# Moving the attention-times-values products one group later and laying the step of a fused transformer block out anew

## The reference, cut to what matters

```python
# x: (16, 56, 56, 32) f32; windows of 7 x 7 after a roll by 3; 4 heads of 8
q, k, v = split(ln(x) @ w_qkv + b_qkv); q = q * 8 ** -0.5      # ln over the 32 channels
attn = softmax(q @ k.T) + bias[head] + mask[window]            # the bias comes after the softmax
x = x + (attn @ v) @ w_proj + b_proj                           # rolled back
probs = softmax(ln(x) @ router_w + router_b)                   # 8 experts
top_p, top_i = top_k(probs, 2); top_p = top_p / sum(top_p)
x = x + sum over the 2 picked experts e of top_p[e] * (ln(x) @ expert_w[e] + expert_b[e])
```

## Time and profile before

| what | value |
|---|---|
| median of 3 runs | 817.04 us (816.79, 817.04, 819.18) |
| the profiled execution: its time | 821.02 us |
| its span, first to last instruction | 819.2 us |
| mean granted clock of TensorE in it | 0.940 of full speed |
| busy in the span | PE 83%, DVE 66%, POOL 63%, PEld 54%, ACT 47% |

### The profile page before, as it was taken

One profiled execution on the slowest core, in us unless ns is written; L12 is line 12 of the kernel. 1 busy time (PEld: TensorE's weight loads), 2 busy tenths in 40 slices (PEclk: granted clock), 3 DMA queues, 4 the chain that ended last, 5 costly groups with the idle time before them and its releaser, 6 DMA issues.

```text
span 819.2 us, 29441 instructions
## 1 busy us (share of the span) xinstructions
PE 677.5 (83%) x12632; PEld 443.1 (54%) x12632; DVE 544.2 (66%) x1003; ACT 387.3 (47%) x641; POOL 516.6 (63%) x555
## 2 busy tenths in 40 slices
PE   0777877979798989989798989989897989878675
PEld 0455554656556655645656565656556556645331
DVE  7352557867676767758676767768686667676544
ACT  1645462646464564636454554646464455612100
POOL 4736677586867768584868767685857666551520
PEclk9999898999999999979999999999998999987777
DMA  2000030313122130413131130413131030403040
GB/s 71 20 22 3 25 77 22 81 42 81 32 62 51 38 85 23 91 32 80 33 70 42 42 82 22 97 26 81 42 82 41 22 81 10 93 2 80 20 99 20
DMA packets 16961, 41.48 MB, mean 51 GB/s; under 512 B 9280, under 2 KB 9408, under 8 KB 15296
## 3 DMA queue, kind: packets, MB, share of 16 engines
q1 hardware_dynamic: 16240, 38.59, 21.2%
q10 hardware_dynamic: 592, 1.01, 0.4%
HBM read 7.47 MB, written 6.42 MB: 17 GB/s over the span
## 4 chain that ended last, share of the span: by engine, by line
PE 56%; DVE 23%; issue 11%; ACT 5%; POOL 4%; ACTq 0%; DVEq 0%; POOLq 0%
DVE mx L874 8%; PE ps_win L1210 7%; PE ps_acc L1310 6%; PE ps_shared L1136 6%; PE ps_weight L1293 5%; PE ps_win L1181 5%; PE ps_pv L1225 5%; PE ps_shared L1163 5%; PE ps_shared L1246 4%; DVE zt L989 4%; PE ps_shared L1147 3%; PE ps_win L1204 3%; DVE x L915 2%; DVE ms L888 2%; PE ps_acc L1305 2%
## 5 line engine op out<-in xcount | busy, mean ns | idle before, releaser
L874 DVE TENSOR_REDUCE mx<-ps_win 128x32 f32<-128x1568 f32 x64 | 114.5, 1789 | 66.5 <-PE ps_win L1181 65.9
L989 DVE TENSOR_TENSOR zt<-ps_weight,x 128x392 f32<-128x392 f32 x118 | 66.2, 561 | 83.0 <-PE ps_weight L1293 82.4
L1225 PEld LDWEIGHTS ps_pv<-vb,pt 128*49 128x49 f32 x4096 | 103.4, 127 | 14.5 <-issue 12.1
L777 ACT ACTIVATE pt<-ps_win 128x1568 f32<-128x1568 f32 x64 | 94.6, 1478 | 33.0 <-PE ps_win L1210 32.5
L611 POOL TENSOR_TENSOR on<-on,obs 128x256 f32<-128x256 f32 x64 | 46.6, 728 | 98.2 <-DVE on L901 72.6
L1225 PE MATMUL ps_pv<-vb,pt 128*49 128x18 f32 x4096 | 108.3, 200 | 0.0
L1293 PE MATMUL ps_weight<-wt,const_bf_tile 96*128 96x392 bf16 x234 | 82.3, 352 | 28.0 <-DVE zt L989 19.5
L989 DVE TENSOR_TENSOR x<-ps_weight,x 128x392 f32<-128x392 f32 x116 | 65.5, 564 | 33.3 <-PE ps_weight L1293 32.3
L768 ACT COPY mr<-ps_win 128x512 bf16<-128x512 bf16 x64 | 37.4, 584 | 87.7 <-PE ps_win L1189 87.7
L590 POOL TENSOR_TENSOR st<-st,minus_half 112x28 f32<-112x28 f32 x16 | 77.0, 4812 | 1.3
L557 POOL TENSOR_TENSOR st<-st,minus_half 112x28 f32<-112x28 f32 x16 | 76.9, 4809 | 1.3
(11 more groups left out here) (141 smaller groups left out, 1369.1 us busy)
## 6 DMA issues: line engine op xcount, KB each, us to landing
x<-x SPq DMA_DIRECT2D x48, 392.0 KB, 5.1
x<-x2t SPq DMA_DIRECT2D x64, 98.0 KB, 2.2
xin<-x SPq DMA_DIRECT2D x32, 150.0 KB
out<-xo SPq DMA_DIRECT2D x32, 150.0 KB
xin<-x SPq DMA_DIRECT2D x32, 18.0 KB
out<-xo SPq DMA_DIRECT2D x30, 18.0 KB
xin<-x SPq DMA_DIRECT2D x32, 15.6 KB
xin<-x SPq DMA_DIRECT2D x32, 1.9 KB
```

What stands on the lines that cost most here:

```text
L777: nc.scalar.activation(pt[g % 2].rearrange("p a x h n -> p a (x h n)"), ps_win[:, :, 0:2 * HN], ACT.Exp).then_inc(probs_ready, 1)
L874: nc.vector.tensor_reduce(mx[g % 2].rearrange("n a x h -> n a (x h)"), ps_win[:, :, 0:8 * N].rearrange("n a (k m) -> n a k m", m=N), AX, A ...
L989: nc.vector.tensor_tensor(tokens if eh else zt[:, a, :], weight_bank(w, 1 + i)[:, 0:HALF], tokens, ALU.mult).then_inc(weight_drained, 1)
L1225: ins = mm(ps_pv[PAD * x:PAD * x + N, c0:c0 + SLOT], pt[g % 2][:, a, x, h, :], vb[u.par][:, 2 * g + x, a, h, :], start=True, stop=True)
```

## The change

The values' products of group g-1 are put between the scores of group g and the next maximum; those of group 3 go into the next unit's first group, and the last unit's stand ahead of the tail. The place (g, 1) is now behind these products, (g, 2) behind the maximum. The work in `SIDE_TASKS` and in `TAIL` is dealt out anew. `ps_acc` becomes a second shared bank: nine of the users (`ON_ACC`) and the two sums take turns on it, and each waits only for the user before it on its own bank. The sum of the experts, which had the bank to itself, now waits for that user too. No instruction is added or left out, and none changes its shape.

```diff
@@ the places of the side work
-    (0, 0): [("ot", 1), ("keep", 0), ("wt", 0), ("y", 0), ("mix", 0), ("back", 0), ("mix", 1), ("y", 1), ("back", 1), ("norm2_center", 0)],
-    (0, 1): [("xt", 0), ("mix", 2)],
-    (0, 2): [],
-    (0, 3): [("mix", 3), ("norm2_square", 0), ("xt", 1), ("mix", 4), ("norm2_scale", 0)],
-    (1, 0): [("qk", 0), ("load", 0), ("mix", 5)],
-    (1, 1): [("qk", 1), ("mix", 6)],
-    (1, 2): [],
-    (1, 3): [("mix", 7), ("qk", 2)],
-    (2, 0): [("mix", 8), ("x2t", 0), ("norm1_center", 0), ("mix", 9)],
-    (2, 1): [("x2t", 1), ("mix_drain", 0)],
-    (2, 2): [("replicate", 0), ("kmask", 0), ("mix", 10), ("router", 0), ("mix", 11), ("qk", 3), ("place", 0), ("mix", 12), ("place", 1)],
-    (2, 3): [("top2", 0), ("mix", 13), ("kmask", 1), ("top2", 1), ("v", 0), ("top2", 2)],
-    (3, 0): [("top2_exp", 0), ("mix", 14), ("top2", 3), ("v", 1), ("mix", 15), ("top2", 4)],
-    (3, 1): [("top2", 5), ("mix", 16), ("ob", 0), ("mix_drain", 1)],
-    (3, 2): [],
-    (3, 3): [("norm1_square", 0), ("final", 0), ("top2", 6), ("top2", 7), ("ot", 0), ("final", 1), ("ob", 1), ("store", 0), ("norm1_scale", 0)],
+    (0, 0): [],
+    (0, 1): [("wt", 0), ("ot", 1), ("mix", 0), ("y", 0), ("back", 0), ("y", 1), ("back", 1), ("norm2_center", 0)],
+    (0, 2): [("xt", 0), ("xt", 1), ("qk", 0), ("mix", 1)],
+    (0, 3): [("norm2_square", 0), ("qk", 1), ("mix", 2), ("keep", 0)],
+    (1, 0): [("norm2_scale", 0), ("mix", 3)],
+    (1, 1): [("load", 0), ("kmask", 0), ("mix", 4)],
+    (1, 2): [("qk", 2), ("mix", 5)],
+    (1, 3): [("norm1_center", 0), ("mix", 6)],
+    (2, 0): [("mix", 7), ("x2t", 0), ("mix", 8)],
+    (2, 1): [("mix", 9)],
+    (2, 2): [("norm1_square", 0), ("mix_drain", 0), ("x2t", 1), ("mix", 10), ("qk", 3), ("router", 0), ("mix", 11), ("v", 0)],
+    (2, 3): [("top2", 0), ("mix", 12), ("place", 0), ("norm1_scale", 0), ("mix", 13), ("mix", 14)],
+    (3, 0): [("top2", 1), ("replicate", 0), ("mix", 15), ("top2", 2)],
+    (3, 1): [("place", 1), ("mix", 16), ("mix_drain", 1)],
+    (3, 2): [("v", 1), ("final", 0), ("ot", 0), ("top2_exp", 0)],
+    (3, 3): [("kmask", 1), ("top2", 3), ("top2", 4), ("top2", 5), ("final", 1), ("top2", 6), ("ob", 0), ("store", 0), ("ob", 1), ("top2", 7)],
@@ the banks
+SUM_STARTS = {5: 0, 13: 1}
+ON_ACC = {("ot", 1), ("xt", 1), ("qk", 0), ("y", 1), ("ot", 0), ("qk", 3), ("qk", 1), ("v", 0), ("ob", 1)}
@@ the tail
-TAIL = ((1, 1), (0, 1), (1, 6), (0, 1), (1, 1), (0, 11), (1, 2), (0, 1), (1, 1), (0, 1), (1, 1), (0, 1), (1, 3), (0, 1), (1, 1), (0, 2), (1, 2), (0, 4), (2, 2), (1, 1), (2, 5), (1, 1), (2, 5), (1, 1), (2, 12))
+TAIL = ((0, 1), (1, 1), (0, 1), (1, 7), (0, 12), (1, 3), (0, 2), (1, 1), (0, 2), (1, 1), (0, 1), (1, 1), (0, 1), (1, 3), (0, 3), (1, 1), (2, 1), (1, 2), (2, 4), (1, 1), (2, 19))
@@ macro_step
         yield "scores", att, g
         yield from side((g, 0))
+        unit, k = (att, g - 1) if g else (post, GROUPS - 1)
+        if unit is not None:
+            yield "pv", unit, k
+        yield from side((g, 1))
         unit, k = (att, g + 1) if g + 1 < GROUPS else (ahead, 0)
         if unit is not None:
             yield "maximum", unit, k
-        yield from side((g, 1))
-        yield "pv", att, g
         yield from side((g, 2))
@@ program, behind the last macro step
+    yield "pv", unit[UNITS - 1], GROUPS - 1
@@ TensorE: the wait before a bank is filled again
-            def shared_free(name, u, i):
+            def bank_free(name, u, i):
...
+                    if on_acc(other, j) != on_acc(name, i):
+                        continue
...
+                    if other == "sum":
+                        pe.wait_ge(sum_drained, upto("sum_drained", w, j))
+                        return
@@ TensorE: the start of a sum in mix
                 if eh == 0:
-
+                    if w.number >= UNITS - 2:
+                        tail_banks_free()
+                    else:
+                        bank_free("sum", w, half)
```

More of the change, by code:

```diff
@@ L97, with bank_order, on_acc @@
+def bank_order():
+    for place in sorted(SIDE_TASKS):
+        for name, i in SIDE_TASKS[place]:
+            if name in SHARED_BANK:
+                yield name, i
+            elif name == "mix" and i in SUM_STARTS:
+                yield "sum", SUM_STARTS[i]
+BANK_ORDER = list(bank_order())
+def on_acc(name, i):
+    return name == "sum" or (name, i) in ON_ACC
 PROLOGUE = (
@@ L474, in metaformer_block, with shared_bank, ot_bank @@
         rel_list = list(rel_loads())
+        def shared_bank(name, i):
+            return ps_acc if on_acc(name, i) else ps_shared
+        def ot_bank(u, i):
+            return ps_shared if u.number == UNITS - 1 and i else shared_bank("ot", i)
         def pre_bank(v, fill):
-            return ps_weight if v.number == 0 and fill % 2 else ps_shared
+            if v.number == 0:
+                return ps_weight if fill % 2 else ps_shared
+            return shared_bank(*PRE_NAMES[fill])
         def weight_bank(w, fill):
@@ L489, in token_bank @@
         def token_bank(w, fill):
-            spare = w.number == UNITS - 1 and fill in (1, 3)
-            return ps_win[:, 3, :] if spare else ps_shared
+            if w.number == UNITS - 1:
+                return ps_win[:, 3, :] if fill in (1, 3) else ps_shared
+            return shared_bank(*TOKEN_NAMES[fill])
         block = ctx.enter_context(nc.Block())
@@ L1093, in keep_awake @@
                     mm(ps_win[:, 0, :], identb, const_bf16_tile[:, 0:512], start=True, stop=True)
-            def shared_free(name, u, i):
-                at = SHARED_ORDER.index((name, i))
-                for back in range(1, 2 * len(SHARED_ORDER)):
-                    lap, k = divmod(at - back, len(SHARED_ORDER))
-                    before, j = SHARED_ORDER[k]
-                    w = u.moved(lap - later(name, i) + later(before, j))
-                    if w is not None:
-                        kind, first = SHARED_BANK[before]
-                        drained = {"pre": pre_drained, "ot": ot_drained, "token": token_drained}[kind]
+            def bank_free(name, u, i):
+                at = BANK_ORDER.index((name, i))
+                for back in range(1, 2 * len(BANK_ORDER)):
+                    lap, k = divmod(at - back, len(BANK_ORDER))
+                    other, j = BANK_ORDER[k]
+                    if on_acc(other, j) != on_acc(name, i):
+                        continue
+                    w = u.moved(lap - later(name, i) + later(other, j))
+                    if w is None:
+                        continue
+                    if other == "sum":
+                        pe.wait_ge(sum_drained, upto("sum_drained", w, j))
+                        return
+                    kind, first = SHARED_BANK[other]
+                    drained = {"pre": pre_drained, "ot": ot_drained, "token": token_drained}[kind]
+                    if kind == "pre" and w.number == 0:
+                        pe.wait_ge(pre_drained, upto("pre_drained", w))
+                    else:
@@ L1112, in token_free @@
                 else:
[L1113 removed]
+                    pe.wait_ge(token_drained, upto("token_drained", w, 3 if name == "router" else 1))
             def pre_free(v, i, fill):
@@ L1265, in router @@
             def router(w, _):
-                shared_free("router", w, 0)
+                token_free("router", w, 0)
+                bank = token_bank(w, 4)
                 pe.wait_ge(token_drained, upto("token_drained", w, 3))
                 for k in range(WS):
-                    ins = mm(ps_shared[0:ROWS, 32 * k:32 * k + 32], x2t[:, ROWS * k:ROWS * k + ROWS],
+                    ins = mm(bank[0:ROWS, 32 * k:32 * k + 32], x2t[:, ROWS * k:ROWS * k + ROWS],
                              wr[:, :, :].rearrange("p a e -> p (a e)"), start=True, stop=True)
```

33 lines of the change are left out of this document (22 added, 11 removed).

## The result

The changed kernel takes **921.4 us** in the median of 4 runs (910.17 to 927.36) against 817.12 before: 1.1228 times as long, interval 1.1171 to 1.1286. The direction was forecast, the size was not: 104 us longer instead of 6, far outside the range of 807 to 836. The ratio compares the means of the fast executions and leaves out the profiled one of the changed kernel, the slowest of its four (927.36 us, span 925.6, mean granted clock 0.869 for 0.881 and more in the others). Set against the span before, 819.2, the profiled execution is 106.4 longer, and the starts of the macro steps split that up: first start 0.9 earlier, units 0 and 1 together 100.3 for 80.2 (**+20.1**), units 2 to 14 673.0 for 594.1 (**+78.9**, 6.1 per step), from the start of unit 15 on 114.7 for 106.4 (**+8.3**).

What follows compares the result with a forecast made beforehand. The prediction took PE (TensorE) as the bound, busy 39.28 and 39.71 us of steps of 44.24 or 44.87. Steps +10.4, head -4 and tail -0.5 gave +5.9 on the median 817.04: 823.0 us, range 807 to 836.

Steps and rivals of the forecast that it cites:

- with 1.79 and the split the shift comes at 12.05: Group 0 on DVE: `mx` starts near 9.4, takes 1.79, then the split; PE waits 0.6 for DVE.
- three losses again: Clock: three of the 13 steps lose the full rate as before, with 4.66 us for one such step.
- The clock is lost more often: Rival, chance 0.10: idle stretches of group 0 follow one another, three more steps lose 4.66 us each, 837 us.
- The walk: One step in the new order with old durations: groups 0 to 3 +0.7, -0.4, +0.7, -0.2; +0.8 us per step.
- The queues: Engine queues that steps are moved past: POOL at worst 0.3 us late, priced at nothing, 13 x 0.5 in the range.
- the late picking: POOL's last picking step ends 4 us into the next step, where `wt` needs it; priced at nothing.
- The load: SP issues it 14 us into the step; it lands at about 20, just ahead of its reduction at about 20.3.
- The banks: Second shared bank: beyond the 0.25 us of `y` 1 it takes away no wait; priced at 0.
- The head: Units 0 and 1, without `mix`: products help in the exponentials' wait; -4 us, from -7 to 0.
- The tail: End of the kernel: `y` 2.3 us later, filling matmuls some 1.8 earlier; -0.5 us in all, from -3 to +3.

Runs made afterwards that it cites:

- run 1: The changed kernel with one wait added, so that POOL's `keep` starts only after DVE's split of group 1's maxima: 866.77 us, ratio 1.0594.
- run 2: The kernel before with `keep` held back until `mx` of group 1 is taken, so it starts with the split: 899.69 us, ratio 1.0978.
- run 7: The kernel before with users moved to the sum's bank: five users 850.78 us, ratio 1.0383; `y` 1 alone 828.90, ratio 1.0101.
- run 4: The changed kernel with maximum 1 ahead of `wt`, `ot` and `y`: 834.11 us; its last kernel, with `keep` also waiting for the split: 831.38.

## Why the prediction was right or wrong

**The step that failed** is in group 0: "with 1.79 and the split the shift comes at 12.05". It took the split at its old duration. The change put `keep` behind the step in which POOL takes the mean out for the second norm (L614), on top of the split, and I costed `keep` only as a place in POOL's queue. The second half of the split took 2.09 us for 0.30, and PE waited 2.61 where I had 0.6. Run 1 takes this away and run 2 brings it about; the share of the loss that goes with it rests on run 1. The old trace showed it at 44.05, in a row next to those that I had picked.

**The clock.** That I took "three losses again" was the second failure, and it more than doubled the first. "The clock is lost more often" had 0.10 and three more losses; in truth all 13 steps lost. In the changed kernel a step of the parity of 45.76 takes 50.44: 1.8 us for the longer split (2.09 for 0.30), and 2.9 more, of which 2.4 are PE's longer busy time (41.63 for 39.24). The 4.66 that the prediction took for one lost clock was no pure price of the clock either: in the step from 346.15 the split met POOL as well (L579 at 356.70, 1.74 us), and again in group 1 (0.67 at 369.36):

```profile
357.00 1.54 DVE L888 TENSOR_SCALAR ms<-mx 128x32 bf16<-128x32 f32 x1
```

I had argued that steps with the same 5 us of idle time ran at 1.00 too. That is so, but those were spread in pieces of 1.13 us and less; in the step shown here the piece of 2.61, and the row of 1.06, 0.29 and 0.32 ahead of `y` 0, were each followed by matmuls at half the rate. The Trainium skill's rule ("TensorE: Matmul & The Clock Gate", HAM oscillation) that idle stretches between groups of matmuls send TensorE back agrees with that, better than with the trace of before.

**The walk, step by step.** In run 1's clean step, against 12.63, 8.30, 12.84 and 10.47 in the step of before that it answers to, group 0 is 13.27 (+0.64; forecast +0.7), group 1 7.82 (-0.48; -0.4), group 2 13.67 (+0.83; +0.7), group 3 11.00 (+0.53; **-0.2**). Three hold. Group 3 doesn't: PE waits 0.69 ahead of `final`, 0.29 for the split and 0.21 for the residual sum, 1.2 us where I had 0.6. Its split is long too (0.73 and 0.59 for 0.24 and 0.30, run 1's timeline): POOL's addition (L648, 0.72 us from 402.02) and placing (L640, from 402.87) run at the same time. It is the step that failed in group 0 over again, in small. So the order costs 1.5 us per step, not 0.8.

**The queues.** That the late picking is level with the chain of group 0 held: `ot` waits 0.29 more for the addition that stands behind the picking on POOL. The last picking part ends 3.7 us into the step (forecast 4) and holds `wt` for 1.06. The load landed in time: DVE waited for `xin` once, 4.5 us for the very first loads, as before (4.61).

**The banks**, priced at nothing but the 0.25 of `y` 1: the 0.25 is won and given back at the split (run 7). In the old order five users cost more, by the sum's wait for its bank (9.2 us in 13 times) and the collision behind it; the changed order has no such wait, so there the price of nothing held.

**The head** (-4 forecast, +20 measured) is the worst term beside the collision. Group 0 of unit 0 has no old products to fill the wait for the exponentials (still 1.57 us), and both `xt` wait for a norm that comes late only in the head. In run 1, without the collision, it is 84.8 us, and in the last kernel of run 4 88.1, for 80.2 before; kernels with the same instructions there differ by 8 to 9 us from one profile to another (100.3 and 92.3, 84.8 and 93.8), so what else holds it was not settled. **The tail** (-0.5; measured +8.3): the lateness of `y` and the filling came out as walked. Much of the rest runs at half clock; I did not test its parts.

Of the 104 us, then, 55 go with the collision and 35 with the order of group 0 (taken in this order, each with the clock that it costs, and in the medians). The 14 that are left are, by the profiled executions, 8 in the head, no more than the profiles differ there, and 3 each in the steps between and in the tail.

## What to carry to other kernels

When a step is moved on GpSimd, look at what VectorE executes in the same microseconds, not only at the queue: a duration from the old trace holds only beside the old neighbours. In the old trace, look for the same instruction with two durations; the longer one names the neighbour to keep it from. And where TensorE is the bound, a new wait of 2 us in one piece costs more than its length: here 1.8 us more on the split went with 4.7 us on the step.

## What the runs showed of the hardware

- A GpSimd `tensor_tensor` of 112x896 f32 with both inputs in SBUF (2.11 us) holds up VectorE instructions that read SBUF alone: the split's second half with two inputs went from 0.30 to 2.09 and 2.14, its first half with one input from 0.24 to 0.95, 1.01 and 1.71 (the last in the head of the changed kernel). The held instruction ends 0.16 or 0.10 us after the GpSimd one, however much it had left to do. GpSimd's own time stays at 2.1. The norm's product (1.70), the step that takes the mean out (1.74), the addition (0.72) and the placing (0.59) do the same. This agrees with the rule of the Trainium skill ("SBUF — State Buffer", two separate sides) that the port pair which the two engines share is an exclusive lock: the one that starts first keeps it for the whole instruction.
- Not every GpSimd instruction does it. During the power of 4.80 us on 112x28 (376.66) the same two halves took 0.24 and 0.30, although both inputs of the power are in SBUF; the rule that the lock is kept for the whole instruction does not explain this row. The reduction out of PSUM (`mx`) took 1.78 or 1.79 in all 64 cases of every run, and in the changed kernel the 234 instructions of 128x392 with one input in PSUM (L1024) took 0.55 to 0.57.
- Behind a stall of 2.61 us on TensorE the granted clock was at 1.2 GHz from about 414 to 417 us, and behind 1.67 us of idle time in three pieces from about 404 to 407; the step took 50.44 us for 45.76. Five filling matmuls in the smaller hole cost nothing in a clean step (45.74) and won 10 us over the kernel, once the larger hole was gone.
